# Restacking K and Q through DRAM in whole rows, with a rewritten prologue, in a gated cross-attention block

## The reference, cut to what matters

```
n  = layernorm(x)                                  # 32 x 112 x 256
q, k, v = n @ wq + bq, ctx @ wk + bk, ctx @ wv + bv   # ctx: 32 x 375 x 256
a  = softmax(q k^T / 4) v, per head;  x = x + tanh(g0) * (a @ wo + bo)
h  = gelu(layernorm(x) @ w1 + b1) @ w2 + b2
x  = x + tanh(g1) * h * s      # s: the sum of the two normalized router weights of a token
```

## Time and profile before

| | |
|---|---|
| three runs | 732.95 to 735.40 us, median 734.27 us |
| the profiled execution | 734.14 us, of which the span of instructions is 732.1 us |
| PE busy | 696.4 us (95% of the span) |
| DVE, ACT, POOL busy | 514.4, 402.5, 321.3 us |
| mean granted PE clock | 0.991 of full speed |
| moved by DMA | 103.21 MB, 141 GB/s on average |

### The profile page before, as it was taken

The page is one execution under the profiler, slowest core; times in us unless marked ns, Lnnn a source line. Parts: engine busy times, 40 slices in busy tenths (PEclk is TensorE's granted clock), DMA queues, the critical chain, the costliest instruction groups (busy, mean ns, idle before and its releaser), DMA issues.

```text
span 732.1 us, 20618 instructions
## 1 busy us (share of the span) xinstructions
PE 696.4 (95%) x7648; PEld 652.3 (89%) x7648; DVE 514.4 (70%) x1298; ACT 402.5 (55%) x800; POOL 321.3 (44%) x476
## 2 busy tenths in 40 slices
PE   3688999999999999999999999999999999999987
PEld 2566888999999999999999999999999999988966
DVE  6378788777776777776777777777677777766422
ACT  2124666465564646556564746556474655656753
POOL 4313436444434545434344544343454543424246
PEclk9979999999999999999999999999999999999999
DMA  4868789866748585764658486684758576450000
GB/s 146 179 198 169 187 189 224 155 170 137 178 104 174 125 187 132 171 167 124 158 111 206 103 187 154 129 190 110 165 122 182 139 171 150 104 93 3 15 1 27
DMA packets 84021, 103.21 MB, mean 141 GB/s; under 512 B 9589, under 2 KB 79570, under 8 KB 83922
## 3 DMA queue, kind: packets, MB, share of 16 engines
q1 hardware_dynamic: 83282, 101.12, 59.9%
q10 hardware_dynamic: 640, 0.77, 0.5%
HBM read 65.05 MB, written 34.05 MB: 135 GB/s over the span
## 4 chain that ended last, share of the span: by engine, by line
PE 87%; DVE 4%; ACT 2%; issue 2%; POOL 2%; SPq 1%; DMA 1%; ACTq 0%; POOLq 0%; DVEq 0%
PE P L921 42%; PE S L951 13%; PE T L963 11%; PE OT L978 11%; PE P L1004 4%; PE TR L987 2%; PE TR L1060 1%; DVE NEGM L764 1%; PE TR L1043 1%; ACT PROBS L678 1%; PE TR L994 1%; PE TR L936 1%; DVE XN L832 1%; PE TR L1028 1%; DMA QS<-q_parts 1%
## 5 line engine op out<-in xcount | busy, mean ns | idle before, releaser
L764 DVE TENSOR_REDUCE NEGM<-S 112x1 f32<-112x375 f32 x512 | 267.3, 539 | 73.4 <-PE S L951 71.3
L678 ACT ACTIVATE PROBS<-T 125x448 f32<-125x448 f32 x384 | 196.2, 543 | 106.0 <-PE T L963 98.4
L951 PE MATMUL S<-KS,QS 96*112 96x376 f32 x512 | 181.7, 361 | 9.6 <-DVE NEGM L764 6.3
L963 PE MATMUL T<-QS,KS 98*125 98x224 f32 x768 | 150.6, 282 | 3.1 <-ACT PROBS L678 1.7
L963 PEld LDWEIGHTS T<-QS,KS 98*125 98x125 f32 x768 | 129.3, 188 | 10.0 <-ACT PROBS L678 4.6
L582 POOL CAST HT_HI<-HG 128x224 fp32r<-128x224 f32 x128 | 47.3, 369 | 152.0 <-ACT HG L701 144.0
L951 PEld LDWEIGHTS S<-KS,QS 96*112 96x112 f32 x512 | 91.3, 180 | 23.5 <-DVE NEGM L764 13.0
L566 POOL CAST CT_HI<-CTRAW 128x750 fp32r<-128x750 f32 x31 | 25.1, 810 | 161.7 <-DMA CTRAW<-in_ctxT 151.0
L584 POOL TENSOR_TENSOR HT_LO<-HG,HT_HI 128x224 fp32r<-128x224 f32 x128 | 85.2, 666 | 10.3
L978 PE MATMUL OT<-PROBS,VA 125*17 125x112 f32 x3072 | 87.6, 260 | 0.0
L701 ACT ACTIVATE HG<-P,B 128x224 f32<-128x224 f32 x128 | 57.2, 447 | 53.4 <-PE P L921 52.2
(11 more groups left out here) (113 smaller groups left out, 1496.8 us busy)
## 6 DMA issues: line engine op xcount, KB each, us to landing
KS<-k_parts SPq DMA_DIRECT2D x90, 375.0 KB, 7.1
CTRAW<-in_ctxT SPq DMA_DIRECT2D x32, 375.0 KB, 3.5
k_parts<-KHI SPq DMA_DIRECT2D x30, 375.0 KB, 3.9
k_parts<-KLO SPq DMA_DIRECT2D x30, 375.0 KB, 4.5
QS<-q_parts SPq DMA_DIRECT2D x96, 112.0 KB, 4.9
X<-in_x SPq DMA_DIRECT2D x16, 224.0 KB, 3.6
q_parts<-QHI SPq DMA_DIRECT2D x32, 112.0 KB, 2.4
q_parts<-QLO SPq DMA_DIRECT2D x32, 112.0 KB, 2.3
```

The costliest lines, as they stand in the source:

```text
L678: act.activation(PT[0:KN, k, pp * 4 * SQ:(pp + 1) * 4 * SQ], T_BANK[i % 2][0:KN, 0:4 * SQ], ACT.Exp, scale=SCALE).then_inc(exp_done, 1)
L764: dve.tensor_reduce(NEGM[:, b.par, i:i + 1], S_BANK[i % 2][0:SQ, 0:SK], AX.X, ALU.max, negate=True).then_inc(max_done, 1)
L951: pe.matmul(S_BANK[i % 2][0:SQ, 0:SKP], QS[0:96, i, b.ring * SQ:(b.ring + 1) * SQ], KS[0:96, b.ring, i // 2, :], start=True, stop=True).th ...
L963: mm = pe.matmul(T_BANK[i % 2][0:KN, r * 2 * SQ:(r + 1) * 2 * SQ], KS[0:98, prv.ring, pair, k * KN:(k + 1) * KN], QS[0:98, 2 * pair:2 * pa ...
```

## The change

Both copies of K in DRAM become 32 rows of 8 x 376 elements, so that a row of KS is one contiguous run; KHI and KLO get a 376th column. The low part moves to partitions 0 to 31, and the two copies of the high part, now in neighbouring partitions 32 to 95, are written by one load that reads its source twice. Q's copies become 16 rows of 8 x 224 elements and QS is laid out by group, half and pair. Heads get another order in VA and in the rows of WO. The prologue's loads and memsets become words (`ld`, `zp`, `zq`, `zo`, `zh`, `zi`, `zr`, `zy`, `zv`); the memset of KS's last column, of ZR and of WT go. W1 and W2 come in eight pieces of 128 x 512 through HG (`lw`, `w`) and POOL makes their low parts, and that of WV. The lists -2 to 5 are new; `ORDER` and the lists from 32 on stay.

```diff
+    (-2, """zq zp zh ld.0 zi l1 wk xn cx ct ld.3 wq ld.2 ld.7 xt k.0 k.1 wv zv zo lw.0 ka.1 q.0 l1-2 zr q.1 zy
+       ld.5 ka.2 v.0 ld.1 ld.6 tg xn-2 ld.4 v.1 cl+1 xt-2 q.0-2"""),
+    (-1, """k.0 q.1-1 k.1 v.2+1 xl-1 wl w.0 v.0 l1-3 v.1 v.2 qs+1"""),
+    (0, """s.0 s.1 ka.2+1 s.2 s.3 s.4 kd.0+2 ql+1 s.5 s.6 s.7 s.8 s.9 s.10 cl+2 kd.1+1 lw.1 ct+1 on+1 s.11 w.1
+       k.0 s.12 s.13 k.1 s.14 v.0 kd.0+1 s.15 v.1 s.0-1 cl+1"""),
...
-        QS = sb("QS", [128, NH, RING * SQ], F32R)
-        KHI = sb("KHI", [128, DC, SK], F32R)
-        KLO = sb("KLO", [128, DC, SK], F32R)
+        QS = sb("QS", [128, 2, 2, NPAIR, TOK], F32R)
+        KHI = sb("KHI", [128, DC, SKP], F32R)
+        KLO = sb("KLO", [128, DC, SKP], F32R)
...
-        KD = nc.dram_tensor("k_parts", (2, 2, NPAIR, 32, SK), F32, kind="Internal").ap()
-        QD = nc.dram_tensor("q_parts", (2, 2, DC, 4, DH, TOK), F32, kind="Internal").ap()
+        KD = nc.dram_tensor("k_parts", (2, 2, 32, NPAIR * SKP), F32, kind="Internal").ap()
+        QD = nc.dram_tensor("q_parts", (2, 2, DH, NPAIR * TOK), F32, kind="Internal").ap()
...
-                        sp.dma_start(QS[r0:r0 + DH, hh:NH:2, cols].bitcast(F32),
-                                     QD[part, hh].rearrange("c p r n -> r (c p) n")).then_inc(qs_loaded, 16)
+                        sp.dma_start(QS[r0:r0 + DH, g.gpar, hh, :, :].bitcast(F32),
+                                     QD[part, hh].rearrange("r (g n) -> r g n", g=NPAIR)).then_inc(qs_loaded, 16)
...
-                        sp.dma_start(KD[nn.par, 0].rearrange("(c p) r n -> (p r) c n", c=DC),
+                        sp.dma_start(KD[nn.par, 0].rearrange("r (p n) -> p r n", p=4),
                                      KHI[:, :, :].bitcast(F32)).then_inc(khi_stored, 16)
...
-                        for row in (0, 2):
-                            sp.dma_start(KS[32 * row:32 * row + 32, nn.ring, :, 0:SK].bitcast(F32),
-                                         KD[nn.par, 0].rearrange("g r n -> r g n")).then_inc(ks_loaded[nn.par], 16)
+                        sp.dma_start(KS[32:96, nn.ring, :, :].rearrange("p g n -> p (g n)").bitcast(F32),
+                                     KD[nn.par, 0].unsqueeze(0).to_broadcast([2, 32, NPAIR * SKP])
+                                     ).then_inc(ks_loaded[nn.par], 16)
                         held(sp, sp_passed, (klo_stored, stored))
-                        sp.dma_start(KS[32:64, nn.ring, :, 0:SK].bitcast(F32),
-                                     KD[nn.par, 1].rearrange("g r n -> r g n")).then_inc(ks_loaded[nn.par], 16)
+                        sp.dma_start(KS[0:32, nn.ring, :, :].rearrange("p g n -> p (g n)").bitcast(F32),
+                                     KD[nn.par, 1]).then_inc(ks_loaded[nn.par], 16)
...
-                            sp.dma_start(QD[0, hh].rearrange("c p r n -> (p r) c n"),
+                            sp.dma_start(QD[0, hh].rearrange("r (p n) -> p r n", p=4),
                                          QHI[64 * hh:64 * hh + 64, :, :].bitcast(F32)).then_inc(qhi_stored, 16)
...
-            dve.memset(KS[:, :, :, SK:SKP].bitcast(F32), 0.0).then_inc(dve_zeroed, 1)
...
+                    if op == "w":
+                        _, raw_in, high, low = w_part(i)
+                        pool.wait_ge(w_split, 2 * i + 1)
+                        pool.tensor_tensor(low, raw_in, high.bitcast(F32), ALU.subtract).then_inc(w_split, 1)
+                        latest[0] = (w_split, 2 * i + 2)
```

More of the change, by code:

```diff
@@ L626, in step @@
                         act.activation(parts[0][:, :, :], raw_in, ACT.Copy).then_inc(split, 1)
-                    if op == "w2":
-                        part = w2_part(i)
-                        act.wait_ge(w2_loaded, 16 * (i + 1))
-                        act.activation(W2[0][:, part, :], W2_IN[:, 0:part.stop - part.start, :],
-                                       ACT.Copy).then_inc(w2_split, 1)
+                    if op == "w":
+                        _, raw_in, high, _ = w_part(i)
+                        act.wait_ge(w_loaded, 16 * (i + 1))
+                        act.activation(high, raw_in, ACT.Copy).then_inc(w_split, 1)
                     if op == "ka":
-                        act.wait_ge(klo_done if i == 1 else khi_done, nn.count(2, 2))
+                        act.wait_ge(klo_done if i == 0 else khi_done, nn.count(2, 2))
                         move_k(act, nn, i)
@@ L730, in step @@
                     bank = P_BANK[BANKS.get((now.k, stage), 0)]
-                    if op in SPLIT:
+                    if op == "zp":
+                        for part in CT:
+                            dve.memset(part[:, :, :, SK:SKP].bitcast(F32), 0.0).then_inc(pads_zeroed, 1)
+                    if op == "zq":
+                        dve.memset(QS[:, 0, 1, :, :].bitcast(F32), 0.0).then_inc(qs_high_zeroed, 1)
+                    if op == "zo":
+                        dve.memset(OT[:, :], 0.0).then_inc(ot_zeroed, 1)
+                    if op in SPLIT and op in LOW_ON_DVE:
                         raw_in, parts, _, split = SPLIT[op]
@@ L1053, in step @@
                     if op == "rt" and pg.exists:
-                        take("TR", lg_done, pg.group(1, 2))
+                        take("TR", lg_done, pg.group(1, 1))
                         if pg.k == 0:
@@ L1068, in step @@
                             if pg.k == 0 and i == 0:
-                                pe.wait_ge(w2_split, 8)
-                            take(p, y_done, pg.group(GB, i + 1 + GB))
+                                pe.wait_ge(w_split, 12)
+                            take(p, y_done, pg.group(GB, i + 1))
                             pe.wait_ge(htlo_done, pg.group(FC, FC // 2))
                         else:
+                            if pg.k == 0 and i == 0:
+                                pe.wait_ge(w_split, 16)
                             pe.wait_ge(htlo_done, pg.group(FC, FC))
```

241 lines of the change are left out of this document (134 added, 107 removed).

## The result

The change made the kernel slower: a median of 1046.3 us in four runs (1041.84 to 1048.54), against 734.36 us for the kernel before beside it. The ratio is 1.4242, with a 95% interval of 1.4187 to 1.4297. The forecast was 990 us, inside a range of 718 to 1100.

What follows compares the result with a forecast made beforehand. PE's work bounds the middle now; after the change, the fullest DMA engine would: 49.7 - 5 + 30 x (27.6 + 1.0) + 86 = 989 us of span, plus 2.0 us around it, forecast 990 us, range 718 to 1100.

Steps and rivals of the forecast that it cites:

- The middle is set by PE's work of 20.4 us a batch, until a transfer is slower: From 120.0 to 639.7 us PE idles 0.2 us; only a transfer slower than 20.4 us a batch changes the middle.
- Engines by the outermost count: K, Q transfers: at worst only 4 engines for stores, 2 for the high load; chance 0.60, 990 us.
- the 900 us for partly different engines: Lower end of the worst case's range, if high load and stores partly use different engines: 900 us.
- 27.6 us a batch on the fullest engine: Worst-case DMA work on the most loaded engine: high load 14.8, K's stores 7.4, Q's stores 2.2, all else 3.2 us.
- a hand-over of 1.0 us: Latency between K's store and its load, added to each batch: 1 us, bounds 0 and 3.
- 7.5 for all sixteen: Best-case DMA work per batch if every transfer uses all sixteen engines: 7.5 us, against 20.4 us of PE work.
- Idle PE released by DMA into KS and QS: Sign in the profile after: PE busy clearly under 90%, its idle time ended by transfers into KS and QS.
- The clock, to which nothing was added: PE waiting about 7 us a batch runs partly at 1.2 GHz, using up waiting time first; nothing added.
- Only the broadcast load confined: 755 us: Rival for the middle: one engine has 20.4 us a batch, just PE's own; 755 us (730 to 850), chance 0.08.
- All sixteen: 726 us: Rival: all sixteen engines serve every transfer, PE sets the middle, the fill gains 8 us; 726 us (717 to 740), chance 0.27.
- The fill: first S at about 29 us, 8 us gained: Prologue: first S 5 us earlier, 3 us of later idle taken; sum -8 us, from +6 to -17.
- POOL's subtractions, which I feared: Fill rival: POOL's subtractions or the eight chained pieces reach `up` late; 740 us, upper bound of the all-sixteen case.

Runs made afterwards that it cites:

- both_wide: Changed kernel with K's and Q's DRAM copies reordered and the high load split in two, so no K or Q transfer has an outermost count under 16: 726.0 us.
- pair_stores: Changed kernel with the broadcast load split into two loads and each K store cut into two of outermost count 2: 1014.6 us.
- wide_stores: Changed kernel with each K store cut into four stores of 32 rows, the broadcast load and Q's stores kept: 921.5 us.
- m_on_act: Changed kernel with the rows `m` of QS issued by ACT on its own queue, no longer by SP behind X's load: 1048.4 us.
- only_broadcast: wide_stores with Q's stores wide too, so the broadcast load is the only confined transfer of K and Q: 920.7 us.
- early_out: Changed kernel with one word of ORDER moved, so SP issues the output's store ahead of the broadcast load: 1010.7 us.
- early_out_wide: wide_stores with one word of ORDER moved, so the output's store is issued ahead of the broadcast load: 876.9 us.

## Why the prediction was right, point by point

- **The middle is set by PE's work of 20.4 us a batch, until a transfer is slower.** Right, and both_wide shows it from the other side: 513.00 us of PE in the 513 us from 120 to 633.
- **Engines by the outermost count.** Right: 32 of 64 and 32 of 128 packets on one engine, the recovery in both_wide, the loss in pair_stores. The load and the stores fill the same engine, so the 900 us for partly different engines falls away. The rule cited from the Trainium skill, "DMA: Bandwidth & Descriptors", section "Why a DMA increments its semaphore by 16 and not by 1", held here, and so did the warning of a leading zero-stride broadcast in its section "Rules for kernel authors" (52 GB/s). In pair_stores an ordinary outermost dimension of 2 in K's stores cost more than the broadcast load does in wide_stores (1014.6 us for 921.5).
- **27.6 us a batch on the fullest engine, and a hand-over of 1.0 us.** The forecast was 28.6 us a batch and the period was 30.7. From the first K store to the last, 49.1 to 938.2 us, that makes 29 x (30.66 - 28.6) = +60 us; the first store came 4.4 us later than forecast, and from the last store to the end it took 101.8 us for 114.6, -13. Together +51, which is the difference of the spans (1040 for 989).
- **Which term was mis-sized.** The 27.6, not the hand-over. In the steady batches the engine worked for 30.3 us and idled for 0.1: K's latency was covered almost wholly, and the 1.0 us stood by luck where part of the missing work was. The missing 2.7 us are mostly the high load, 16.0 us for 14.8, and K's stores, 8.3 for 7.4. The prediction priced every byte at the 26 GB/s that an engine showed in one large load. The earlier trace rows already said otherwise: a DMA share of 0.66 at 151 GB/s is 14 GB/s for a busy engine, and 13.5 us a batch where the prediction had 7.5 for all sixteen. On the full engines, which often work beside few others, the gap was smaller, and that is why the forecast was near.
- **Idle PE released by DMA into KS and QS.** Half right: QS (138.6 us), and never KS. The prediction named the right queue behind the wait but not the output's store in it. Where PE waits doesn't matter much, as m_on_act shows (0 us).
- **The clock, to which nothing was added.** The granted clock was 0.856, as forecast (under 0.95), and PE's own work took 68 us more. That it lay in waiting time, as the prediction argued, fits an engine queue without idle time in the middle; no run measures it.
- **Only the broadcast load confined: 755 us.** Wrong, 921 us (only_broadcast). Of the 6.2 us a batch that were missing, 4.4 are work priced too low and 1.8 an idle queue, while wide transfers that stand behind the load are waited for. The forecast of 990 has the first error, by less, and hardly the second.
- **All sixteen: 726 us.** The rival didn't happen. Its price was met to the microsecond, 726.0 us in both_wide, and in part by luck, as the next point says.
- **The fill: first S at about 29 us, 8 us gained.** The gain was right as a sum (8 to 9 us), its steps weren't. The first S was later, at 37.6 us. The new list puts more of K, V and Q ahead of it, which wasn't tested by itself, and the memsets hold up DVE. The gain came from the filled time: in both_wide PE is busy for 98.5 of the first 120 us, in the kernel before for 94.3. POOL's subtractions, which I feared, weren't tested by themselves; they left the sum of the fill a gain.

## What to carry to other kernels

Before reshaping a transfer into longer runs, look at the outermost dimension of both sides: here, counts of 2 and 4 cost 320 us (1046 for 726), and runs of 3 KB over all sixteen engines kept PE busy throughout. When a transfer fills a few engines, price its bytes at less than the best rate of one engine, and look at the share of busy time beside the GB/s in the kernel before. Wide transfers behind it are late as well, since each has a part on the full engines. A chain of waits through a queue doesn't yet show that the waits set the pace. Ask first whether the fullest engine ever stands idle: where it doesn't, removing the largest wait can be worth nothing (m_on_act), and moving one word can be worth no more than it changes in the packets' speed (early_out).

## What the runs showed of the hardware

- **An issue can block.** In the steady state of the changed kernel, SP needed 10.12 us to issue one load of 224 KB, for 0.34 us in wide_stores (at 414.16 us), and all its later transfers waited. The row stands where K's stores of outermost count 4 had just been queued behind the broadcast load. In early_out the same issue takes 5.94 us and stands in the chain (SPq L544, 7%), in pair_stores some 4 us, and in only_broadcast and early_out_wide, whose K stores are wide, 0.33 us again. That the queues of the few full engines had no room left is my reading; no run measures their depth.
- **A confined transfer loads its engines unevenly, and an engine slows beside others.** One engine carried 32 of the 64 packets of 12032 bytes of the high load and 2 of the 32 of the low load. Such a packet took 0.45 us with one other engine at work, and up to 1.4 us with all sixteen (431 to 434 us in the changed kernel).
- **DVE beside POOL's memset.** Two normalizations that take 0.74 us together took 4.91 us beside POOL's two memsets of QS (1.59 and 3.08 us). The kernel before has the same at 61.90 us: 3.04 us, beside a memset of KS on POOL of 2.60 us. Keeping them apart was worth 5 us. The Trainium skill, "SBUF — State Buffer", section "Who interferes with whom", has the rule: DVE, in a mode that takes a second pair of ports, and GpSimd shut each other out for a whole instruction, and the second to issue waits. The trace agrees: DVE's row ends 0.5 us after the memset does. In which mode the normalizations ran, it doesn't say.
